# Cross-attention on one NeuronCore: who splits the query and key projections into three bf16 parts

## The chip, the cores and the metric

The kernel runs on one core of one Trainium2 chip. The metric is the time of one execution on the device in microseconds (us). Five engines work side by side, each through its own list of instructions in order: PE (TensorE, matrix products, with its weight loads shown apart as PEld), DVE (VectorE), ACT (ScalarE), POOL (GpSimd) and SP (SyncE, which here only issues DMAs). They meet at semaphores: an instruction may wait until a semaphore has reached a value, and raises one when it ends.

## What is computed

Four cross-attentions share one query: 128 batch elements, 128 queries and 128 keys each, 320 channels in 20 heads of 16. The keys of an element fall into four segments (77, 4, 4 and 43 long), each with its own key and value weights and its own softmax.

```python
q = _heads(hidden_states @ to_q_w)
h_txt = _sdpa(q, _heads(ehs_txt @ to_k_w), _heads(ehs_txt @ to_v_w))
h_obj = _sdpa(q, _heads(ehs_obj @ to_k_object_w), _heads(ehs_obj @ to_v_object_w))
h_oth = _sdpa(q, _heads(ehs_oth @ to_k_others_w), _heads(ehs_oth @ to_v_others_w))
h_ip = _sdpa(q, _heads(ehs_ip @ to_k_ip_w), _heads(ehs_ip @ to_v_ip_w))
out = _merge(h_txt) + _merge(h_obj) + _merge(h_oth) + _merge(h_ip)
out = out @ to_out_w + to_out_b + residual
```

`_sdpa` is softmax(q k^T / 4) v per head.

## The kernel before

**Groups and slots.** Four batch elements form a group (32 groups); the 80 heads of a group are taken eight at a time, an octet, in ten slots. PE, DVE, ACT and POOL each have a function `slot(g, n)` that writes out by hand what the engine does in slot n of group g, and `groups` runs it over all groups. In slot n PE computes the scores of octet n+2 (L824), transposes the probabilities of octet n-2 in two halves into one of two ring banks (L851), multiplies values (L864) and projects the output, which the text calls y (L871). DVE takes maxima, subtracts them, sums the exponentials and inverts the sums (L624, L640, L667, L678). ACT takes the exponentials (L541) and copies the transposed probabilities out of the ring (L550). POOL scales the probabilities (`scale`, L463 and L466).

**Projection jobs.** Beside this PE works twelve jobs a turn (`SEQ`) into two PSUM banks that alternate (`job_ps`): q0 to q2 (queries), kv0 to kv4 (keys, then values) and v0 to v3 (transposes). `PIECES` says in which slot a job or half of one is put: kv0 ends in slot 7, kv1 begins in slot 8, in the same bank. `wait_bank` (L756) makes PE wait until that bank has been read. The jobs q0, q1, q2, kv0, kv1, kv2 (`SPLITS`) of a turn belong to the group two turns later, the other jobs to the next one.

**The three parts.** Queries and keys are multiplied in bf16, each value as a sum of three bf16 parts. For each of the six split jobs of a turn:

- ACT, in `evacuate` (L505): rounds the bank to the first part (L523), and raises `part1_made`. It first waits until the parts buffer, one of three, has been stored (`parts_stored`, L522).
- DVE, in `subtract_part` (L649): bank minus first part into `rest` (L657), and raises `part_freed`, which is what PE waits for (L763) before it writes the bank again.
- POOL, in `split` (L436): adds zero to `rest`, rounded to the second part (L444), then subtracts that for the third part (L447), and raises `part3_made`.
- SP, in `store_parts` (L311): waits for `part3_made` and issues three DMAs that store the parts in DRAM scratch. `load_pair` (L324) waits until all six stores of a group are in, then loads the stacked operands of half a group into `q_all` and `k_all`.

A job that ends in slot m at place 0 (`at` is 0 in `ENDS`) is evacuated by ACT in slot m, one at place 1 in slot m+1; DVE subtracts in slot m+1 and POOL splits in slot m+2, at either place.

**The start.** Before the groups every engine goes through `EARLY_JOBS`: the six split jobs of turn -2 (for group 0), then the twelve jobs of turn -1: kv3, kv4, q0, v0, q1, v1, q2, v2, kv0, v3, kv1, kv2 (splits for group 1). SP's list there, in order: the loads, the stores of the parts 0 to 2 of group 0, `w_o`, the stores of the parts 3 to 5 (L371), `load_pair(0, 0, 0)` (L373), the load of the next context (`load_c(1)`, L374), the store of `small_scr`, 2.6 MB of small key segments (L376), `load_small(1)`, which waits until that store has landed (L378), `load_pair(0, 0, 1)` (L379), two residual loads, `load_x(2)`, and the stores of the parts 0 to 3 of group 1 (L383).

Of the kernel before, what the change touches and what calls it, by code (L numbers as in the profile page):

```python
# [14 lines left out]
P = 128  # L15
# [24 lines left out]
N_CONSTS = 5  # L40
# [85 lines left out]
def split_rows(n):  # L126
    return CT if SPLITS[n][1] == 2 else P
# [7 lines left out]
def xattn_kernel(nc: bass.Bass, x, xT, cT, cT_small, wq, wk, wv, wko, wvo, wkt, wvt, wki, wvi, wo, bo, out):  # L135
# [13 lines left out]
    with ExitStack() as stack:  # L149
# [23 lines left out]
        zero = sb("zero", [P, 1])  # L173
        parts = sb("parts", [P, PR, 3, NB * S], bf16)
        rest = sb("rest", [P, 2, NB * S])
# [45 lines left out]
        part_freed = sem("part_freed")  # L221
        copy_freed = sem("copy_freed")
        part1_made = sem("part1_made")
        part2_made = sem("part2_made")
# [198 lines left out]
        def _(pool):  # L423
# [3 lines left out]
            pool.memset(zero[:, :], 0.0).then_inc(consts_made, 1)  # L427
# [8 lines left out]
            def split(g, n):  # L436

                r = split_rows(n)
                src, dst = rest[0:r, n % 2, :], parts[0:r, n % PR, :, :]
                pool.wait_ge(part_freed, g * NSP + n + 1)  # L440

                after(pool, parts_stored[n % PR], (g * (NSP // PR) + n // PR) * STORED)

                pool.tensor_tensor(dst[:, 1, :], src, zero[0:r, :].broadcast_to((r, NB * S)), ALU.add)\  # L444
                    .then_inc(part2_made, 1)
                pool.wait_ge(part2_made, g * NSP + n + 1)
                pool.tensor_tensor(dst[:, 2, :], src, dst[:, 1, :], ALU.subtract).then_inc(part3_made, 1)  # L447
# [30 lines left out]
            for n in range(3):  # L478
                split(0, n)
            for k in range(CX):  # L480
                x_low(1, k)
            for n in range(3, NSP):
                split(0, n)
            for n in range(NSP):
                split(1, n)
# [3 lines left out]
            def slot(g, n):  # L489

                if live(g * NO + n - 1, G * NO):
                    scale(g if n else g - 1, (n - 1) % NO)
                for at in range(2):
                    for turn, job in ended(g, n - 2, at):
                        if job in SPLITS:
                            split(turn + 2, SPLITS.index(job))
                for k in range(CX):
                    if XLO_AT[k] == n and live(g + 3, G):
                        x_low(g + 3, k)
# [4 lines left out]
        def _(act):  # L504
            def evacuate(turn, job):  # L505

                kind, i = job
                g = turn + shift_of(job)
                ps = job_ps[bank_of(turn, job)]
                act.wait_ge(job_filled, job_count(turn, job))  # L510
                if kind == "v":

                    after(act, v_spread, (g - 1) * NB + i + 1)
                    act.activation(v_new[:, i, :], ps[:, P - CT:3 * P], ACT.Copy).then_inc(copy_freed, 1)
                elif job in COPIES:
                    act.activation(vT[:, i - 2, :, :], ps[:, :].rearrange("p (b t) -> p b t", b=NB), ACT.Copy)\
                       .then_inc(copy_freed, 1)
                else:
                    m = SPLITS.index(job)
                    r = split_rows(m)  # L520

                    after(act, parts_stored[m % PR], (g * (NSP // PR) + m // PR) * STORED)  # L522
                    act.activation(parts[0:r, m % PR, 0, :], ps[0:r, :], ACT.Copy).then_inc(part1_made, 1)  # L523
                    if job == ("kv", 2):

                        act.activation(vT[CT:P, 0, :, :], ps[CT:P, :].rearrange("p (b t) -> p b t", b=NB), ACT.Copy)\
                           .then_inc(v_head_copied, 1)

# [48 lines left out]
            act.wait_ge(pads_made, N_PADS)  # L577
            for turn, job in EARLY_JOBS:
                evacuate(turn, job)
                if (turn, job) == (-2, ("q", 2)):  # L580
                    for k in range(CX):
                        x_high(1, k)
            spread(0, 0)
# [4 lines left out]
            def slot(g, n):  # L588
# [3 lines left out]
                for turn, job in ended(g, n - 1, 1):  # L592
                    evacuate(turn, job)
                for at, (nn, kind, what) in enumerate(FILLS):
# [19 lines left out]
        def _(dve):  # L614
# [34 lines left out]
            def subtract_part(turn, job):  # L649

                g, m = turn + 2, SPLITS.index(job)
                r = split_rows(m)
                ps = job_ps[bank_of(turn, job)]
                dve.wait_ge(part1_made, g * NSP + m + 1)

                after(dve, part3_made, g * NSP + m - 1)
                dve.tensor_tensor(rest[0:r, m % 2, :], ps[0:r, :], parts[0:r, m % PR, 0, :], ALU.subtract)\  # L657
                   .then_inc(part_freed, 1)

# [44 lines left out]
            for turn, job in EARLY_JOBS:  # L704
# [8 lines left out]
                if job in SPLITS:  # L713
                    subtract_part(turn, job)
# [5 lines left out]
            def slot(g, n):  # L720
# [7 lines left out]
                for at in range(2):  # L728
                    for turn, job in ended(g, n - 1, at):
                        if job in SPLITS:  # L730
                            subtract_part(turn, job)
# [10 lines left out]
        def _(pe):  # L742
# [13 lines left out]
            def wait_bank(turn, job):  # L756

                before = previous_in_bank(turn, job)
                if before is not None:
                    t, other = before  # L760
                    g = t + shift_of(other)
                    if other in SPLITS:
                        pe.wait_ge(part_freed, split_count(g, other))  # L763
# [188 lines left out]
```

## Time and profile before

| | |
|---|---|
| median of 3 runs | 1751.53 us (1750.83 to 1751.56) |
| the profiled execution | 1750.32 us |
| its span, first to last instruction | 1748.5 us |
| mean granted clock of PE | 0.990 |
| DMA queue of SP | 365.79 MB, 82.4% of 16 engines' span |

Time is read from the start of the span. A line of the timeline gives start, duration, engine, line and operation, output<-inputs, their shapes and the count, and in brackets the idle time before it with what ended it. A row of waits gives who waited for whom, the total in us, the number of times and the longest.

### The profile page before, as it was taken

Reading aid. Unit: us, or ns where it says so; the run is one execution under the profiler, and the core shown is the slowest. Engines: PE = TensorE matmul, PEld = TensorE weight load, DVE = VectorE, ACT = ScalarE, POOL = GpSimd, SP = SyncE. Lnnn points to the kernel's source line nnn. Section 1 sums busy time; section 2 is a strip of 40 time slices with the busy share of each in tenths; the row PEclk is TensorE's granted clock in tenths of the full one; section 3 lists DMA queues with packets and bytes.
Section 4 is the critical chain, followed back from the end, with each engine's and each line's share of the span. In section 5 each row is a group of like instructions: output and inputs, shape, how many; then the busy total and the mean of one; then the engine's idle time right before and its main releaser. Section 6 shows DMA issues by size and latency. Waiting matters only on the chain.

```text
span 1748.5 us, 48271 instructions
## 1 busy us (share of the span) xinstructions
PE 1663.6 (95%) x15120; PEld 1370.2 (78%) x15120; DVE 1509.1 (86%) x3536; ACT 1042.8 (60%) x1860; POOL 1247.9 (71%) x1452
## 2 busy tenths in 40 slices
PE   6949999999999999999999999999999999999986
PEld 3647888888888888888888888888888888888865
DVE  4238999889999988999998899999889999988997
ACT  1126666666666666666666666666666666666664
POOL 4337777778777777877777887777788777778744
PEclk9979999999999999999999999999999999999999
DMA  8669888888988988898898889889889988987861
GB/s 294 173 168 222 205 221 220 216 219 217 227 201 221 222 215 216 220 224 204 220 224 213 213 222 222 205 222 226 211 213 225 218 208 220 227 209 195 214 128 39
DMA packets 409172, 366.24 MB, mean 209 GB/s; under 512 B 17137, under 2 KB 380210, under 8 KB 404786
## 3 DMA queue, kind: packets, MB, share of 16 engines
q1 hardware_dynamic: 409138, 365.79, 82.4%
q8 instruction: 20, 0.33, 0.1%
q14 instruction: 14, 0.11, 0.0%
HBM read 216.30 MB, written 149.42 MB: 209 GB/s over the span
## 4 chain that ended last, share of the span: by engine, by line
PE 88%; DVE 5%; issue 2%; DMA 1%; ACT 1%; SPq 1%; POOL 1%; ACTq 0%; POOLq 0%
PE job_ps L785 30%; PE ring_ps L851 15%; PE ring_ps L871 12%; PE ring_ps L864 10%; PE job_ps L801 7%; PE s_ps L824 7%; PE job_ps L804 2%; PE ring_ps L752 2%; PE job_ps L812 2%; DVE rest L657 1%; PE job_ps L795 1%; DVE l_seg L667 1%; ACT parts L523 1%; DVE probs L640 1%; DVE m_seg L624 1%
## 5 line engine op out<-in xcount | busy, mean ns | idle before, releaser
L463 POOL TENSOR_TENSOR probs<-probs,rl 128x616 f32<-128x616 f32 (+1 forms) x640 | 628.5, 1004 | 342.1 <-DVE rl L678 340.8
L785 PE MATMUL job_ps<-c_in,w_kv 128*128 128x172 f32 (+1 forms) x2560 | 576.7, 368 | 40.8 <-DVE rest L657 40.8
L550 ACT ACTIVATE pT<-ring_ps 128x512 f32<-128x512 f32 x640 | 378.2, 598 | 356.1 <-PE ring_ps L851 347.3
L785 PEld LDWEIGHTS job_ps<-c_in,w_kv 128*128 128x128 f32 x2560 | 424.4, 190 | 129.8 <-DVE rest L657 48.4
L851 PE MATMUL ring_ps<-ident,probs 128*128 128x128 f32 x2560 | 388.7, 277 | 9.7 <-DVE y L687 8.4
L667 DVE TENSOR_REDUCE l_seg<-probs 128x8 f32<-128x616 f32 (+1 forms) x640 | 385.2, 644 | 7.8 <-ACT probs L541 7.8
L640 DVE TENSOR_TENSOR probs<-s_ps,m_seg 128x616 f32<-128x616 f32 (+1 forms) x640 | 387.5, 647 | 0.0
L624 DVE TENSOR_REDUCE m_seg<-s_ps 128x8 f32<-128x616 f32 (+1 forms) x640 | 371.6, 623 | 3.5 <-issue 0.2
L541 ACT ACTIVATE probs<-probs 128x1024 f32<-128x1024 f32 x320 | 337.7, 1055 | 22.8 <-DVE probs L644 22.8
L851 PEld LDWEIGHTS ring_ps<-ident,probs 128*128 128x128 f32 x2560 | 290.0, 143 | 64.9 <-issue 25.6
L444 POOL TENSOR_TENSOR parts<-rest,zero 128x512 bf16<-128x512 f32 (+1 forms) x192 | 199.0, 1036 | 70.6 <-DVE rest L657 70.6
L657 DVE TENSOR_TENSOR rest<-job_ps,parts 128x512 f32<-128x512 f32 (+1 forms) x192 | 131.4, 684 | 127.0 <-ACT parts L523 127.0
L871 PE MATMUL ring_ps<-w_o,oT 128*128 128x320 f32 x768 | 231.9, 438 | 5.7 <-ACT pT L550 5.0
L447 POOL TENSOR_TENSOR parts<-rest,parts 128x512 bf16<-128x512 f32 (+1 forms) x192 | 222.3, 1158 | 15.0
L824 PE MATMUL s_ps<-k_all,q_all 128*128 128x128 bf16 x2560 | 196.0, 219 | 6.4 <-DVE probs L644 6.4
L824 PEld LDWEIGHTS s_ps<-k_all,q_all 128*128 128x128 bf16 x2560 | 165.4, 101 | 42.3 <-issue 27.5
L864 PE MATMUL ring_ps<-pT,v_pad 128*32 128x128 f32 x5120 | 194.8, 277 | 0.0
L871 PEld LDWEIGHTS ring_ps<-w_o,oT 128*128 128x128 f32 x768 | 135.8, 190 | 53.1 <-ACT pT L550 11.6
L864 PEld LDWEIGHTS ring_ps<-pT,v_pad 128*32 128x32 f32 x5120 | 159.8, 110 | 14.1 <-issue 0.8
L557 ACT ACTIVATE oT<-ring_ps 128x256 f32<-128x256 f32 x128 | 49.2, 384 | 199.3 <-PE ring_ps L864 195.7
L523 ACT ACTIVATE parts<-job_ps 128x512 bf16<-128x512 f32 (+1 forms) x192 | 113.5, 591 | 86.4 <-PE job_ps L795 44.7
L801 PE MATMUL job_ps<-x_hi,w_q 128*128 128x512 f32 x384 | 145.6, 420 | 19.5 <-POOL x_lo L452 15.4
(47 smaller groups left out, 1457.0 us busy)
## 6 DMA issues: line engine op xcount, KB each, us to landing
q_all<-q_scratch SPq DMA_DIRECT2D x64, 960.0 KB, 8.4
k_all<-k_scratch SPq DMA_DIRECT2D x64, 960.0 KB, 12.4
c_in<-in_cT SPq DMA_DIRECT2D x32, 1024.0 KB, 5.1
x_raw<-in_xT SPq DMA_DIRECT2D x32, 768.0 KB, 5.1
q_scratch<-parts SPq DMA_DIRECT2D x64, 384.0 KB, 3.0
k_scratch<-parts SPq DMA_DIRECT2D x64, 384.0 KB, 3.0
x_res<-in_x SPq DMA_DIRECT2D x128, 160.0 KB, 3.4
out<-y SPq DMA_DIRECT2D x128, 160.0 KB, 2.8
```

Source lines behind the costliest of these rows:

```text
L463: pool.tensor_tensor(pr[:, :, a:e], pr[:, :, a:e], r[:, :, s:s + 1].broadcast_to((P, OH, e - a)), ALU.mult)
L541: act.activation(pr, pr, ACT.Exp, scale=SCALE).then_inc(exp_done, 1)
L550: act.activation(pT[:, h:h + QH, :], ring_ps[i][:, :].rearrange("p (h s) -> p h s", h=QH), ACT.Copy)\
L624: dve.tensor_reduce(m_seg[:, o % 2, :, k:k + 1], sc[:, :, a:e], axis=AX.X, op=ALU.max)\
L640: dve.tensor_tensor(pr[:, :, a:e], sc[:, :, a:e], m_seg[:, o % 2, :, k:k + 1].broadcast_to((P, OH, e - a)), ALU.subtract)
L667: dve.tensor_reduce(l_seg[:, o % 2, :, s:s + 1], pr[:, :, a:e], axis=AX.X, op=ALU.add)
L785: last = pe.matmul(dst[:, :, a:e], w_kv[:, l, k, i * P:(i + 1) * P], c_in[:, k, :, a:e], start=(k == 0), stop=(k == CK - 1))
L801: pe.matmul(ps[:, :], w_q[a][:, k, i * P:(i + 1) * P], (x_hi, x_lo)[c][:, k, :], start=(k == 0 and (a, c) == (0, 0)), stop=False)
L824: last = pe.matmul(s_ps[o % 2][:, i * T:(i + 1) * T], q_st[s // 2][:, h, s % 2, :], k_st[s // 2][:, h, s % 2, :], start=True, stop=True)
L851: last = pe.transpose(ring_ps[i][:, k * S:(k + 1) * S], probs[:, (o % NR) * OH + q * QH + k, :], ident[:, :])
L864: last = pe.matmul(ring_ps[i][a * VW:(a + 1) * VW, k * S:(k + 1) * S], v_pad[:, s, h, :], pT[:, (s % 2) * H + h, :], start=(e == 0), stop= ...
L871: last = pe.matmul(ring_ps[i][:, 0:C], oT[:, k, :], w_o[:, k, :], start=(k == 0), stop=(k == 2))
```

## The change

The difference is now taken on POOL, from a copy of the bank that ACT makes in SBUF (`whole`, fp32), and the second part is rounded by ACT. The bank is free as soon as ACT has made the copy and the first part. `split` on POOL becomes `make_rest` and `make_third`, with `round_second` of ACT between them. POOL calls `make_rest` one slot after ACT's evacuation, and `make_third` one slot later, in the same slot as ACT's `round_second`. At the start ACT rounds the second part of a split job after it has evacuated the split job that follows.

```diff
-            def split(g, n):
+            def make_rest(g, n):
                 r = split_rows(n)
-                src, dst = rest[0:r, n % 2, :], parts[0:r, n % PR, :, :]
-                pool.wait_ge(part_freed, g * NSP + n + 1)
-                after(pool, parts_stored[n % PR], (g * (NSP // PR) + n // PR) * STORED)
-                pool.tensor_tensor(dst[:, 1, :], src, zero[0:r, :].broadcast_to((r, NB * S)), ALU.add)\
-                    .then_inc(part2_made, 1)
+                src = whole[0:r, n % 2, :]
+                pool.wait_ge(part1_made, g * NSP + n + 1)
+                pool.tensor_tensor(src, src, parts[0:r, n % PR, 0, :], ALU.subtract).then_inc(rest_made, 1)
+
+            def make_third(g, n):
+                r = split_rows(n)
                 pool.wait_ge(part2_made, g * NSP + n + 1)
-                pool.tensor_tensor(dst[:, 2, :], src, dst[:, 1, :], ALU.subtract).then_inc(part3_made, 1)
+                pool.tensor_tensor(parts[0:r, n % PR, 2, :], whole[0:r, n % 2, :], parts[0:r, n % PR, 1, :],
+                                   ALU.subtract).then_inc(part3_made, 1)
...
-            for n in range(3):
-                split(0, n)
-            for k in range(CX):
-                x_low(1, k)
-            for n in range(3, NSP):
-                split(0, n)
-            for n in range(NSP):
-                split(1, n)
+            for g in range(2):
+                for n in range(NSP):
+                    if (g, n) == (0, 3):
+                        for k in range(CX):
+                            x_low(1, k)
+                    make_rest(g, n)
+                    make_third(g, n)
...
                 for at in range(2):
-                    for turn, job in ended(g, n - 2, at):
+                    for turn, job in ended(g, n - 2 - at, at):
                         if job in SPLITS:
-                            split(turn + 2, SPLITS.index(job))
+                            make_third(turn + 2, SPLITS.index(job))
+                for at in range(2):
+                    for turn, job in ended(g, n - 1 - at, at):
+                        if job in SPLITS:
+                            make_rest(turn + 2, SPLITS.index(job))
...
+                    after(act, part3_made, g * NSP + m - 1)
+                    act.activation(whole[0:r, m % 2, :], ps[0:r, :], ACT.Copy)
+
                     after(act, parts_stored[m % PR], (g * (NSP // PR) + m // PR) * STORED)
                     act.activation(parts[0:r, m % PR, 0, :], ps[0:r, :], ACT.Copy).then_inc(part1_made, 1)
...
+            def round_second(g, m):
+                r = split_rows(m)
+                act.wait_ge(rest_made, g * NSP + m + 1)
+                act.activation(parts[0:r, m % PR, 1, :], whole[0:r, m % 2, :], ACT.Copy).then_inc(part2_made, 1)
...
+            waiting = None
             for turn, job in EARLY_JOBS:
                 evacuate(turn, job)
+                if job in SPLITS:
+                    if waiting is not None:
+                        round_second(*waiting)
+                    waiting = (turn + 2, SPLITS.index(job))
                 if (turn, job) == (-2, ("q", 2)):
                     for k in range(CX):
                         x_high(1, k)
+            round_second(*waiting)
             spread(0, 0)
...
                 for turn, job in ended(g, n - 1, 1):
                     evacuate(turn, job)
+                for at in range(2):
+                    for turn, job in ended(g, n - 2 - at, at):
+                        if job in SPLITS:
+                            round_second(turn + 2, SPLITS.index(job))
...
-                dve.tensor_tensor(rest[0:r, m % 2, :], ps[0:r, :], parts[0:r, m % PR, 0, :], ALU.subtract)\
-                   .then_inc(part_freed, 1)
...
                     if other in SPLITS:
-                        pe.wait_ge(part_freed, split_count(g, other))
+                        pe.wait_ge(part1_made, split_count(g, other))
```

With `subtract_part` its two calls on DVE go, and so do the column `zero` and its memset.

## Rows read from the trace of the kernel before

**Rows 1.** The page, part 1: busy time, share of the span, instructions
```profile
PE 1663.6 (95%) x15120; PEld 1370.2 (78%) x15120; DVE 1509.1 (86%) x3536; ACT 1042.8 (60%) x1860; POOL 1247.9 (71%) x1452
```

**Rows 2.** Who waited for whom, 140 to 1640 us, PE, then PEld
```profile
PE job_ps L785 <- DVE rest L657: 19.8, 29, 0.7
...
PEld ring_ps L871 <- ACT pT L550: 4.8, 30, 0.2
```

**Rows 3.** Timeline of PE, 895 to 955 us: scores of octet 0, kv1, y
```profile
923.47 0.61 PE L824 MATMUL s_ps<-k_all,q_all 128*128 128x128 bf16 x8
...
925.21 2.34 PE L785 MATMUL job_ps<-c_in,w_kv 128*128 128x308 f32 x8 [0.68 <-DVE rest L657]
...
927.82 1.78 PE L871 MATMUL ring_ps<-w_o,oT 128*128 128x320 f32 x6
```

**Rows 4.** The chain that ended last, 0 to 140 us: start, length, what
```profile
74.88 14.07 DMA small_scratch<-probs
...
106.80 0.61 ACT parts L523
...
108.18 5.09 PE job_ps L785 x16
...
122.86 1.12 DVE l_seg L667 x2
```

**Rows 5.** Timeline of POOL, 0 to 135 us: the last third part of group 0
```profile
56.34 1.15 POOL L447 TENSOR_TENSOR parts<-rest,parts 64x512 bf16<-64x512 f32 x1
```

**Rows 6.** Timeline of ACT, 0 to 135 us
```profile
76.43 0.60 ACT L523 ACTIVATE parts<-job_ps 128x512 bf16<-128x512 f32 x1 [1.33 <-PE job_ps L804]
...
117.77 0.59 ACT L523 ACTIVATE parts<-job_ps 64x512 bf16<-64x512 f32 x1 [3.73 <-PE job_ps L795]
...
119.00 0.83 ACT L566 ACTIVATE v_pad<-v_new 128x320 f32<-128x320 f32 x2
...
121.30 1.04 ACT L541 ACTIVATE probs<-probs 128x1024 f32<-128x1024 f32 x1
```

**Rows 7.** Timeline of ACT, 895 to 955 us
```profile
923.35 0.60 ACT L550 ACTIVATE pT<-ring_ps 128x512 f32<-128x512 f32 x1 [1.18 <-PE ring_ps L851]
923.84 0.59 ACT L523 ACTIVATE parts<-job_ps 128x512 bf16<-128x512 f32 x1
924.32 0.63 ACT L535 ACTIVATE x_hi<-x_raw 128x512 fp32r<-128x512 f32 x1
...
926.10 0.61 ACT L550 ACTIVATE pT<-ring_ps 128x512 f32<-128x512 f32 x1
```

**Rows 8.** Timeline of SP, 0 to 135 us
```profile
50.61 8.65 SPq L322 DMA_DIRECT2D k_scratch<-parts  x9
61.13 0.36 SPq L330 DMA_DIRECT2D q_all<-q_scratch  x1
61.53 0.88 SPq L330 DMA_DIRECT2D k_all<-k_scratch  x1
...
74.49 0.35 SPq L295 DMA_DIRECT2D c_in<-in_cT  x1
```

**Rows 9.** Busy time by stretch; the last columns are granted clock, DMA share, GB/s
```profile
65.00:69.00 4.00, 4.00 (x13) 2.15 (x12) 1.39 (x2) 0.00 (x0) 0.00 (x0) 1.00 1.19 203
...
72.00:75.00 3.00, 3.00 (x18) 2.63 (x17) 0.00 (x0) 0.50 (x1) 0.00 (x0) 1.00 0.08 12
75.00:79.00 4.00, 2.92 (x15) 2.17 (x14) 0.69 (x1) 1.02 (x3) 1.09 (x2) 1.00 0.76 225
```

**Rows 10.** Costliest groups of instructions, shapes apart: a subtraction on POOL
```profile
L452 POOL TENSOR_TENSOR x_lo<-x_raw,x_hi 128x512 fp32r<-128x512 f32 x96 | 122.1, 1275 | 55.3 <-ACT x_hi L535 55.2
```

**Rows 11.** Who waited for whom, 140 to 1640 us, all engines
```profile
POOL probs L463 <- DVE rl L678: 293.2, 177, 2.9
```

**Rows 12.** Timeline of SP, 895 to 955 us: a load of the key stack
```profile
901.62 3.26 SPq L330 DMA_DIRECT2D k_all<-k_scratch  x1
```

**Rows 13.** The line L330, 140 to 1600 us: from issue to landing
```profile
DMA to landing us min/median/max: 7.1/10.5/14.0
```

More of the change, by code:

```diff
@@ L39 @@
 N_SMALL = len(SMALL) * MKV
-N_CONSTS = 5
+N_CONSTS = 4
 N_PADS = 6
@@ L172, in xattn_kernel @@
         ident = sb("ident", [P, P])
-        zero = sb("zero", [P, 1])
         parts = sb("parts", [P, PR, 3, NB * S], bf16)
-        rest = sb("rest", [P, 2, NB * S])
+        whole = sb("whole", [P, 2, NB * S])
         q_all = sb("q_all", [P, NPAIR * H * 2 * S], bf16)
@@ L220, in xattn_kernel @@
         job_filled = sem("job_filled")
-        part_freed = sem("part_freed")
         copy_freed = sem("copy_freed")
         part1_made = sem("part1_made")
+        rest_made = sem("rest_made")
         part2_made = sem("part2_made")
@@ L426, in _ @@
                 pool.memset(t[:, :, C:3 * P].bitcast(fp32), 0.0).then_inc(consts_made, 1)
-            pool.memset(zero[:, :], 0.0).then_inc(consts_made, 1)
             pool.memset(ident[:, :], 0.0).then_inc(consts_made, 1)
@@ L647, in shift @@
                    .then_inc(shifted, 1)
[L649 to L656, printed above, removed]
-                dve.tensor_tensor(rest[0:r, m % 2, :], ps[0:r, :], parts[0:r, m % PR, 0, :], ALU.subtract)\
-                   .then_inc(part_freed, 1)
             def sum_up(g, o):
@@ L712, in _ @@
                     reduce_max(0, 0)
-                if job in SPLITS:
-                    subtract_part(turn, job)
             dve.wait_ge(small_stored, 16)
@@ L727, in slot @@
                         add_residual(g + what // NB, what % NB, at % 2)
[L728 to L731, printed above, removed]
                 if live(gg, G):
```

## The prediction

> **What bounds the kernel now.** First the shares of the page: PE is busy 95% of the span, DVE 86%, POOL 71%, ACT 60% [rows 1]. So only what PE waits for can give time back. Second, who waits for whom in the steady part, 140 to 1640 us: PE's matmuls wait for one thing alone, the subtraction on DVE, 29 times and 19.8 us in all, 0.68 us each [rows 2]. The timeline shows the place: in slot 8, kv1 may not write its bank until DVE has read kv0 out of it [rows 3]. This is the largest gain that the steady part can hold: 19.8 us, 1.1% of the time. Third, the start: there the chain runs for long stretches through DMAs and SP's list, not through PE: the store of `small_scr` lands at 74.88 + 14.07 = 88.95 us, what SP has queued behind it brings in the first store of group 1's query parts, and at 106.80 ACT can at last overwrite that buffer, after which DVE subtracts, and PE goes on with kv1 at 108.18 [rows 4]. Anything that makes SP late there is paid in full.
>
> **The change, part by part.** I write the group index first, so (0, 5) is the last split job of group 0.
>
> *A, SP's list at the start.* ACT now rounds the second part of (0, 5) only after it has evacuated the next split job, and that is q0 of the next turn. Before, POOL had its third part at 56.34 + 1.15 = 57.49 [rows 5]. Now ACT's evacuation of q0 begins at 76.43 [rows 6]; whole copy, first part and rounding take, at the spacing of 0.48 between two of ACT's copies [rows 7], 2 x 0.48 + 0.63 = 1.6, so to 78.0; a wake of some 0.05 (the gap between dependent steps of SP, 74.49 + 0.35 to 74.88 [rows 4, 8]) and the subtraction's 1.15 [rows 5] make 79.2. SP's list waits there: in front of it the store of (0, 5), behind it `load_pair(0, 0, 0)`, `load_c(1)`, `small_scr`, `load_small(1)`. Before, the pair was issued 61.13 - 57.49 = 3.64 after the third part [rows 5, 8], so it is now issued at 82.9, 21.8 later. That alone is not the delay, for `load_c` waited until 74.49 for a job of PE [rows 8]. Behind the pair's issue, 61.53 + 0.88 - 61.13 = 1.3 us [rows 8], it now comes at 84.3: 9.8 later. The store of `small_scr` follows directly, and before it found an empty queue: between 72 and 75 us the DMA share was 0.08 [rows 9]. Now the pair's 2 x 960 KB lie in front of it. The pair took from 61.13 to 72.2 (0.08 of the last 3 us), 11.1 us, so now to 94.0. Then the context and `small_scr`, 74.49 to 88.95 before, 14.46; of this some 1.4 was start-up, which the share of 0.76 beside 1.19 in 4 us shows [rows 9], and is hidden when they queue. So the store lands at 94.0 + 13.0 = 107.0, 18.1 later. Bounds: 84.3 + 14.46 = 98.8 if the pair took nothing from it (9.8 later), 108.5 if nothing is hidden (19.5 later). I take 18.1, because the pair kept the engines as full (1.19) as anything does [rows 9].
>
> What follows the store to 106.80 is the same list, loads and buffer: so ACT's first part of kv0 begins at 124.9. PE's kv0 needs the late context too, which by the above is in by some 101, and stays in that shadow.
>
> The Trainium skill ("DMA: Bandwidth & Descriptors", section Bandwidth) puts the HBM side's limit for one core at about 358 GB/s. By that figure the pair's 1.97 MB would be an estimated 5.5 us and the store would land 5.6 earlier than I say. The trace does not agree: the pair moves at 203 GB/s with the engines full [rows 9], and the sum goes by that.
>
> *B, the release of the bank at that point.* The whole copy is made while ACT waits for the buffer. From the start of the first part to PE it was 108.18 - 106.80 = 1.38 [rows 4]; now it is the part's 0.61 and a wake: -0.7.
>
> *C, the end of the start.* After kv2 ACT had first part and a second copy, and went on with `spread` at 119.00, 1.23 after 117.77 [rows 6]. Now it makes whole copy and first part (0.48 more), rounds (1, 4) (0.5 to 0.6), then has to wait for the rest of (1, 5), which POOL makes only after the third part of (1, 4): third 1.15, rest between 1.15 and 1.28 [rows 5, 10], and the wakes; then it rounds (1, 5), 0.6. With wakes 0.48 + 0.6 + 0.05 + 1.15 + 0.05 + 1.2 + 0.05 + 0.5, some 4.0, so the first exponential starts at 125.3 instead of 121.30 [rows 6], counted with all else where it was, and is done 1.04 later. DVE's first sum, at 122.86 and in the chain [rows 4], comes at 126.4: +3.6. At least it is 1.0 (two more copies of ACT), at most 4.0.
>
> *D, the steady slots.* Slot 8: ACT's evacuation of kv0 begins at 923.84 and not sooner, since the copy before it has waited 1.18 for PE [rows 7]. Whole copy 0.48, first part 0.60, wake 0.05: PE is released at 924.97 instead of 925.21, 0.24 less [rows 3, 7]. Behind this ACT copies the ring bank that y needs: it began at 926.10 and took 0.61 [rows 7]; whole copy (0.48) and the rounding of q2 (0.5 to 0.63) now stand ahead of it, so it ends at 927.7 to 927.8, and y, which could start at 927.82 - 0.24 = 927.58 [rows 3], waits 0.1 to 0.25. Net -0.1 to 0.05. Slot 6: y already waits there, once a group, 4.8 us in 30 times [rows 2]; q2's evacuation just ahead has one copy more, of which I take 0.1, for ACT too waits for PE there; the bounds are 0 and 0.48. Together +1 over 30 groups, between -7 (0.24 x 30, nothing given back) and +15.
>
> *What I cost at nothing.* DVE loses 192 subtractions (six a group); DVE is not what PE waits for but at that one place. POOL gets a subtraction (1.15 to 1.28) for an addition, and `make_third` waits in POOL's list for ACT; the octet's `scale` and the `x_low` of slots 8 and 9 queue behind it. POOL idles before `scale` 293 us in 30 groups, near 10 a group [rows 11]; without that cover PE's transposes wait. ACT gets two copies for each split, some 1.1 x 192 = 211 us, and its share becomes some 71%; its waits for `rest` and for the third part of two jobs before are met a slot earlier. On SP, the third parts of jobs that end at place 1 come a slot later, and the stores, the output stores and `load_pair` behind them: the later half of the key stack was issued at 901.62 and lands at most 14.0 later, 915.6 [rows 12, 13]; a slot later (at most 1750.32 / 320 slots = 5.5 us) that is 921.1, and the first scores that read it stand at 923.47 [rows 3]. So that is hidden too, with 2 us to spare.
>
> **Sum**, against the profiled execution of 1750.32: 18.1 - 0.7 + 3.6 + 1.0 = 22.0, so 1772.3. The median of the runs shown is 1.2 above that execution: **1773.5 us**, 1.3% slower.
>
> **The rivals.**
> 1. *The queued transfers overlap.* If the pair costs the store less than its full time, the store lands between 98.8 and 107.0. For it: small and large transfers share the engines. Against it: the share is full while the pair runs [rows 9]. The time is 1751.5 + 9.8 - 0.7 + 3.6 + 1.0 = 1765 at the lower end. By the figure of the Trainium skill that A names, an estimate, it would be 1768.
> 2. *The gap in slot 8 closes altogether* (the other side). Its place is PE's wait before kv1; it decides if ACT's two copies end by 924.5, where PE would otherwise stand, 0.45 sooner than my reading. Price -19.8 [rows 2]. With A at its lower bound and C at 1.0 that gives 9.8 - 0.7 + 1.0 - 19.8 = -9.7, 1742 us. Against it: the copy ahead waits for PE's transposes [rows 7], so nothing can start the two copies sooner.
> 3. *ACT's copies come too late for PE in every group.* In slots 6 and 8 y waits for a ring bank; at 0.5 us a group instead of 0.03 this is +15 in place of +1: 1787.5. For it: both slots are at their limit [rows 2, 7]. Against it: ACT itself waits for PE in them.
> That the change does not do what it says is no rival: the order of ACT's list at the start can be read from the code.
>
> **How the numbers follow.** Forecast 0.60 (1766 to 1780 with its own bounds), rival 1 0.17, rival 2 0.05, rival 3 0.15, and 0.03 for a gain and a loss that cancel. The range has to reach to most of rivals 1 and 3: 1757 to 1788. A measurement of this kernel tells 0.2%, 3.5 us, from no change; faster is rival 2, slower all but rival 2 and the cancelling.
>
> **What would show it.** A: the pair issued near 83 instead of 61.13, `small_scr` landing near 107, kv1's first matmul at 125 to 126. B: kv1 released by ACT's first part. C: first exponential about 7.5 us after kv2's evacuation begins, not 3.5. D: the wait in slot 8 is put down to ACT, 0.4 to 0.5 a group. I am wrong if the pair is issued before 75 us, or if the distance from kv1 at the start to the end of the span changes by over 15 us.

## The result, and the profile after

The changed kernel takes **1766.09 us** (median; 1765.38 to 1766.72), the kernel before 1751.3 beside it: a ratio of 1.0085, 95% interval 1.0067 to 1.0102. That is +14.8 us, where +22.0 was forecast; it lies in the range, on its faster side. The span is 1763.4 us, 14.9 longer than before.

Part 1 of the page after [rows 1]:

```profile
PE 1674.5 (95%) x15120; PEld 1373.2 (78%) x15120; DVE 1393.6 (79%) x3344; ACT 1211.7 (69%) x2244; POOL 1265.9 (72%) x1451
```

The work moved as the diff says: DVE lost 115.5 us of busy time and 192 instructions, ACT gained 168.9 us and 384, POOL 18. And the time grew: at most places PE waits for none of the three. The few where it does come next.

**The start.** Timeline of SP after, 0 to 150 us [rows 8]:

```profile
82.54 0.36 SPq L329 DMA_DIRECT2D q_all<-q_scratch  x1
82.95 0.88 SPq L329 DMA_DIRECT2D k_all<-k_scratch  x1
83.87 5.59 SPq L294 DMA_DIRECT2D c_in<-in_cT  x1
```

The chain that ended last, after, 0 to 140 us [rows 4]:

```profile
77.80 1.17 POOL parts L445
...
89.50 14.76 DMA small_scratch<-probs
...
119.84 0.61 ACT parts L528
...
120.49 5.48 PE job_ps L789 x16
...
139.08 1.21 DVE l_seg L677 x2
```

The pair is issued at 82.54 instead of 61.13, after the late third part of (0, 5) at 77.80. Behind it SP stands 5.59 us in the issue of `c_in` alone, which took 0.35 before [rows 8]: the queue holds the pair. The store of `small_scr` lands at 89.50 + 14.76 = 104.26, 15.3 later than before; kv1 begins 12.3 later (120.49 for 108.18), DVE's first sum 16.2 later (139.08 for 122.86).

Busy time by stretch, after; the last three columns are granted clock, DMA share and GB/s [rows 9]:

```profile
88.00:90.00 2.00, 0.00 (x0) 0.00 (x0) 0.00 (x0) 0.00 (x0) 0.00 (x0) 0.50 1.24 249
90.00:92.00 2.00, 0.00 (x0) 0.00 (x0) 0.00 (x0) 0.00 (x0) 0.00 (x0) 0.50 1.30 252
```

At little more share of the engines (1.24 and 1.30 beside 1.19) the pair now moves at some 250 GB/s, where before it was 203 [rows 9]; from 86 to 88 us it is 270, but the first stretch of a load is the fastest in e1 too (249, then 199). Nothing in the forecast accounts for that. Loads from issue to landing, before and then after (number, KB, us):

```profile
k_all<-k_scratch SPq DMA_DIRECT2D x1, 960.0 KB, 11.7
...
c_in<-in_cT SPq DMA_DIRECT2D x1, 1024.0 KB, 5.9
```

```profile
c_in<-in_cT SPq DMA_DIRECT2D x1, 1024.0 KB, 12.6
...
k_all<-k_scratch SPq DMA_DIRECT2D x1, 960.0 KB, 11.2
```

The pair, whose second half is `k_all`, lands at 82.95 + 11.2 = 94.2, the context at 83.87 + 12.6 = 96.5. So the context comes in 2.3 us behind the pair, where alone it took 5.9, and `small_scr` lands 10.1 us behind the pair.

Timeline of ACT after, 0 to 145 us [rows 6]:

```profile
130.47 0.59 ACT L525 ACTIVATE whole<-job_ps 64x512 f32<-64x512 f32 x1 [2.73 <-PE job_ps L799]
...
135.19 0.63 ACT L538 ACTIVATE parts<-whole 64x512 bf16<-64x512 f32 x1 [2.37 <-POOL whole L439]
...
138.01 1.99 ACT L552 ACTIVATE probs<-probs 128x1024 f32<-128x1024 f32 x2
```

From kv2's evacuation to the first exponential it is 138.01 - 130.47 = 7.54 us, where before it was 3.53; 2.37 of them ACT waits for POOL's last `rest`.

**The steady slots.** Who waited for whom after, 150 to 1655 us (total, times, longest) [rows 2]:

```profile
PE job_ps L789 <- ACT parts L528: 13.0, 29, 0.4
PEld ring_ps L875 <- ACT pT L561: 12.9, 59, 0.2
```

The wait before kv1 fell from 19.8 to 13.0; the wait of y's weight loads for a ring bank rose from 4.8 to 12.9, and comes twice a group instead of once. Timelines of slot 8 after, PE and then ACT [rows 3, 7]:

```profile
939.59 2.34 PE L789 MATMUL job_ps<-c_in,w_kv 128*128 128x308 f32 x8 [0.45 <-ACT parts L528]
...
942.35 1.88 PE L875 MATMUL ring_ps<-w_o,oT 128*128 128x320 f32 x6
```

```profile
937.96 0.60 ACT L561 ACTIVATE pT<-ring_ps 128x512 f32<-128x512 f32 x1 [1.18 <-PE ring_ps L855]
938.46 0.59 ACT L525 ACTIVATE whole<-job_ps 128x512 f32<-128x512 f32 x1
938.93 0.60 ACT L528 ACTIVATE parts<-job_ps 128x512 bf16<-128x512 f32 x1
...
941.19 0.63 ACT L538 ACTIVATE parts<-whole 64x512 bf16<-64x512 f32 x1
941.71 1.29 ACT L561 ACTIVATE pT<-ring_ps 128x512 f32<-128x512 f32 x2
```

ACT's two copies end at 939.53 and PE follows after 0.45 idle (0.68 before); q2's rounding at 941.19 then stands ahead of the ring copy that y reads, and six matmuls of y take 1.88 instead of 1.78. Octets are counted from the start, ten to a group. ACT's exponential of octet 20 begins at 234.40 us for 220.34 before, that of octet 290 at 1614.45 for 1599.33: 14.1 and 15.1 late, so 27 groups cost 1.1 us together. So nearly all of the +14.8 is the start.

In between, group 0 makes some 2 us of the start's 16.2 good: the exponential of octet 10 is 14.0 late (183.29 for 169.27). The waits of PE before, 121 to 180 us, show two that are gone after; that these are what is made good is argued from their size, not shown:

```profile
PE job_ps L801 <- DVE rest L657: 1.9, 1, 1.9
PE job_ps L785 <- DVE rest L657: 0.7, 1, 0.7
```

### The profile page after: what moved, and what is told of

It reads as the page before. It is cut to its first block, busy times and chain, and to the rows that moved or that the text cites. A ratio compares the mean times of both kernels' runs of the same rounds, so it can differ in the third digit from the quotient of the medians.

```text
span 1763.4 us, 48140 instructions
## 1 busy us (share of the span) xinstructions
PE 1674.5 (95%) x15120; PEld 1373.2 (78%) x15120; DVE 1393.6 (79%) x3344; ACT 1211.7 (69%) x2244; POOL 1265.9 (72%) x1451
## 4 chain that ended last, share of the span: by engine, by line
PE 89%; DVE 4%; ACT 2%; issue 2%; DMA 1%; SPq 1%; POOL 0%; ACTq 0%; POOLq 0%
PE job_ps L789 30%; PE ring_ps L855 15%; PE ring_ps L875 12%; PE ring_ps L868 10%; PE job_ps L805 7%; PE s_ps L828 7%; PE job_ps L808 2%; PE job_ps L816 2%; PE ring_ps L756 2%; PE job_ps L799 1%; ACT parts L528 1%; DVE l_seg L677 1%; DMA small_scratch<-probs 1%; DVE probs L661 1%; DVE m_seg L645 1%
## 5 line engine op out<-in xcount | busy, mean ns | idle before, releaser
L445 POOL TENSOR_TENSOR parts<-whole,parts 128x512 bf16<-128x512 f32 (+1 forms) x192 | 222.2, 1157 | 236.9 <-ACT parts L538 233.2
L439 POOL TENSOR_TENSOR whole<-whole,parts 128x512 f32<-128x512 f32 (+1 forms) x192 | 222.1, 1157 | 6.4 <-ACT parts L528 6.4
L875 PEld LDWEIGHTS ring_ps<-w_o,oT 128*128 128x128 f32 x768 | 135.6, 190 | 61.2 <-ACT pT L561 19.7
L525 ACT ACTIVATE whole<-job_ps 128x512 f32<-128x512 f32 (+1 forms) x192 | 113.6, 592 | 81.9 <-PE job_ps L799 64.5
L805 PE MATMUL job_ps<-x_hi,w_q 128*128 128x512 f32 x384 | 144.2, 416 | 17.0 <-DVE oT L705 15.3
L451 POOL TENSOR_TENSOR x_lo<-x_raw,x_hi 128x512 fp32r<-128x512 f32 x96 | 121.9, 1273 | 7.2 <-ACT x_hi L546 7.0
```

The lines of the kernel that those rows point to most:

```text
L805: pe.matmul(ps[:, :], w_q[a][:, k, i * P:(i + 1) * P], (x_hi, x_lo)[c][:, k, :], start=(k == 0 and (a, c) == (0, 0)), stop=False)
L875: last = pe.matmul(ring_ps[i][:, 0:C], oT[:, k, :], w_o[:, k, :], start=(k == 0), stop=(k == 2))
```

## The experiments

Each edit is made to the changed kernel unless another is named. Ratios are to the kernel before, run beside it: it took 1751.3 us beside the change, 1751.38 beside e1 to e4, 1750.49 beside e5 to e8 and 1751.27 beside e9 to e12.

**Why were the loads faster?** The change drops a column `zero` of 4 bytes a partition; what is allocated behind it moves. One kernel keeps it:

```diff
+        zero = sb("zero", [P, 1])      # unused, at its old place
```

> The changed kernel with the unused 4-byte column `zero` still allocated where it was, so that all buffers behind it in SBUF (parts, whole, q_all, k_all, ...) stand as in the kernel before. Nothing else differs. Theory placement: the key and query stack loads were faster after the change (250 to 270 GB/s beside 195 to 203 before at the start) because their destination moved by those 4 bytes. Then here the pair moves at about 200 GB/s again, DMA share in the middle of the kernel is 0.86 instead of 0.78, kv1 starts near 125.5 us instead of 120.5, and the time is about 5 us above the changed kernel's 1766.1, 1771. Rival, traffic: the loads were faster because less else was in the queues at that time. Then the rate stays at 250 to 270 GB/s and the time at 1766.

1770.82 us, 1.0108 (1.0093 to 1.0123): 4.7 slower than the change without it. Stretches, and the chain:

```profile
88.00:90.00 2.00, 0.00 (x0) 0.00 (x0) 0.00 (x0) 0.00 (x0) 0.00 (x0) 0.89 1.18 199
90.00:92.00 2.00, 0.00 (x0) 0.00 (x0) 0.00 (x0) 0.00 (x0) 0.00 (x0) 0.50 1.20 181
```

```profile
90.99 15.86 DMA small_scratch<-probs
...
124.25 0.61 ACT parts L529
```

```profile
k_all<-k_scratch SPq DMA_DIRECT2D x1, 960.0 KB, 12.5
```

The pair is back at 181 to 199 GB/s, so the placement makes the difference in rate. The store lands at 106.85 and ACT's first part of kv0 begins at 124.25; forecast were 107.0 and 124.9. But this execution issued the pair at 83.83, 1.3 later than the change did, and such a difference is found without any move of the buffers (e11, placed like the change and with the same start, issues it at 83.48). So of the 4.4 us between 119.84 and 124.25 some 3.1 are left for the placement. And the agreement with the forecast is made of errors that cancel; the section on why the prediction was right or wrong has them.

Against the kernel before, whose buffers stand at the same places, the change costs 1770.82 - 1751.38 = 19.4 us, and not 14.8.

The reverse: the kernel before, with `zero` allocated behind `y` instead of at its place.

> The kernel before with `zero` allocated behind all other buffers. Nothing else differs. Theory placement: the pair moves at 250 to 270 GB/s, DMA share in the middle 0.78 instead of 0.86; at the start the pair that stands ahead of group 1's first parts takes 2 to 3 us less, kv1 starts near 106 instead of 108.2, and the time falls by 2 to 3 us to 1749; the steady groups keep their 51.07 us, since no engine waits for these loads there. Rival, traffic: the rate stays at 200 GB/s and the time at 1751.3.

1748.85 us, 0.9986 (0.9977 to 0.9995). Stretches, and the chain:

```profile
65.00:69.00 4.00, 4.00 (x13) 2.04 (x12) 1.65 (x2) 0.00 (x0) 0.00 (x0) 1.00 1.25 241
```

```profile
107.13 6.15 PE job_ps L785 x16
...
122.87 1.12 DVE l_seg L667 x2
```

The loads speed up as expected, 241 GB/s where it was 203, but the gain at the start falls short: kv1 comes 1.05 sooner, and DVE's first sum not at all (122.87 for 122.86). The first pair is not waited for here, since `c_in` waits for PE until 74.97 anyway. What the second pair gains is lost to PE's clock: kv1's 16 matmuls take 6.15 us for 5.09 before. Stretches before, then of this kernel (the granted clock is the third number from the end):

```profile
111.00:113.00 2.00, 2.00 (x12) 1.68 (x11) 0.00 (x0) 0.00 (x0) 0.00 (x0) 0.90 0.82 317
```

```profile
111.00:113.00 2.00, 2.00 (x10) 1.82 (x9) 0.00 (x0) 0.00 (x0) 0.00 (x0) 0.62 0.67 252
```

In both PE had been idle, for 19.29 us before and 17.81 here, and began kv1 at a granted clock of 0.50, the lower of its two levels (1.2 GHz); here it stays there longer. The traces of the two kernels end 0.8 us apart (1748.5 and 1747.7), nearly all of it from the steady groups: the exponential of octet 20 is 0.04 sooner, that of octet 290 0.77. The rest of the 2.4 us that the medians show lies in no trace. A faster transfer pays only where it is waited for: in the changed kernel it is. Against this kernel, whose column is out of the way like the change's, the change costs 1766.09 - 1748.85 = 17.2 us.

**Is it the late third part of (0, 5)?** It is rounded at once, before the jobs of turn -1:

```diff
                     waiting = (turn + 2, SPLITS.index(job))
+                if (turn, job) == (-2, ("kv", 2)):
+                    round_second(*waiting)
+                    waiting = None
```

> The changed kernel, but at the start ACT rounds the second part of (0, 5) before it goes on to turn -1, and not after q0 of turn -1. Theory A (SP is held by the store of (0, 5), and all behind it is late): the pair is issued near 66 us instead of 82.5, `small_scr` lands near 89 instead of 104.3, kv1 starts near 105 instead of 120.5, and the time falls by about 15 us to 1751. Rival (the start is late because ACT has two copies more per job and POOL waits for ACT each time): kv1 comes no more than 3 us sooner, and the time stays above 1762.

1751.56 us, 1.0003 (0.9994 to 1.0012): 14.5 of the 14.8 are gone. Timeline of SP:

```profile
66.78 0.36 SPq L329 DMA_DIRECT2D q_all<-q_scratch  x1
...
74.63 0.35 SPq L294 DMA_DIRECT2D c_in<-in_cT  x1
```

The pair is issued before the context's release again, so its issue no longer holds anything up. Part A is nearly the whole loss. Against e2, where the buffers are moved as here, 2.7 us are left (1751.56 for 1748.85), for the parts C and D.

**Is it the issue that is late, or the transfers in front?** The pair is issued behind the store instead of ahead of it: `load_pair(0, 0, 0)` moves from before `load_c(1)` to before `load_small(1)`.

> The changed kernel, but SP issues the first load of the stacks behind the store of `small_scr` instead of ahead of it. Theory queue (what delays group 1's first parts is all that stands ahead of them in one queue, in whatever order): `small_scr` lands some 7 us sooner, near 97, but kv1 starts where it did, 120.5 within 2 us, because the pair now stands in front of the second pair. Rival (the wait for `small_scr` to land is what counts): kv1 starts some 7 us sooner, near 113.5, and the time falls to 1759.

1763.14 us, 1.0063 (1.0048 to 1.0079). Timeline of SP, and the chain:

```profile
83.82 8.34 SPq L329 DMA_DIRECT2D q_all<-q_scratch  x1
```

```profile
82.65 13.81 DMA small_scratch<-probs
...
118.33 6.12 PE job_ps L789 x16
```

The store lands at 96.46, 7.8 sooner, so the pair did stand in front of it. But kv1 comes only 2.2 sooner and the time is 3.0 shorter: the pair then delays what follows, 8.34 us in one issue. In these two runs another order within the full queue shifts the delay, and only the earlier issue (e3) removes it.

**Part C: the last rounding ahead of the first exponential.** `round_second(*waiting)` moves behind the `spread`s and the `x_high` copies.

> The changed kernel, but at the end of the start ACT makes the last rounding, of (1, 5), after the two spreads and the three high parts, not before them. Theory C (ACT waits there 2.4 us for POOL's rest, and the first exponential behind it is late): the wait is gone, the first exponential starts 2.4 us sooner after kv2's evacuation, 5.1 instead of 7.5, and the time falls by 2 to 2.5 us to 1763.8. Rival (the first group makes it up anyway, since DVE has less to do there): the exponential is sooner, but the time stays within 1 us of 1766.1.

1764.27 us, 1.0077 (1.0063 to 1.009): 1.8 less by the medians, 1.0 less against the kernel before beside each, and the two intervals overlap. Timeline of ACT:

```profile
130.15 0.59 ACT L525 ACTIVATE whole<-job_ps 64x512 f32<-64x512 f32 x1 [2.73 <-PE job_ps L799]
...
135.41 1.99 ACT L552 ACTIVATE probs<-probs 128x1024 f32<-128x1024 f32 x2
```

The first exponential begins 135.41 - 130.15 = 5.26 after kv2's evacuation instead of 7.54; some 1.7 over the 3.53 of before stay. But the exponential of octet 20 begins at 233.61 for 234.40, only 0.8 sooner. So what ACT is late here is paid in part, and group 0 makes up the greater part: the result lies between the theory and the rival.

**Part D: q2's rounding ahead of y's ring copy in slot 8.** It moves behind that copy:

```diff
-                        if job in SPLITS:
+                        if job in SPLITS and n != 8:
                             round_second(turn + 2, SPLITS.index(job))
...
+                        if n == 8 and what[1] == 0:
+                            for turn, job in ended(g, n - 3, 1):
+                                if job in SPLITS:
+                                    round_second(turn + 2, SPLITS.index(job))
```

> The changed kernel, but in slot 8 ACT rounds q2's second part behind the first copy out of the ring and not ahead of it. Theory D (kv1 is released 0.23 us sooner in every group, but y in slot 8 then waits for that ring copy, which the rounding has made late): PE's wait for the ring copies, put on its weight loads at 12.9 us in the middle of the kernel, falls to near the 4.8 of the kernel before, a group takes 0.15 to 0.25 us less, and the time falls by 4 to 7 us to 1760.5. Rival (y's ring copy is not what holds PE there): the time stays at 1766.

1759.18 us, 1.0048 (1.0035 to 1.0062): 6.9 less, 6.1 against the kernel before beside each. Waits, 150 to 1655 us:

```profile
PE job_ps L793 <- ACT parts L528: 13.4, 30, 0.4
...
PEld ring_ps L879 <- ACT pT L561: 6.5, 30, 0.2
```

The wait before kv1 stays as it was, the wait of y halves from 59 times to 30. So the gain of the sooner release was really there, 6 to 7 us, and y in slot 8 had taken it.

All three mends together:

> The changed kernel with the three orders mended: the second part of (0, 5) rounded before turn -1 (as in the run that rounds it at once), the last rounding of the start behind the high parts, and slot 8 as in the run on its order. If A, C and D are separate, their gains add: 1751.6 - 2.3 - 5.5, about 1744, 0.4% below the kernel before. If the first group makes C up, 1746; if slot 8 gives nothing, 1749 to 1751.

1743.41 us, 0.9959 (0.9945 to 0.9973). Singly they gave 14.5, 1.8 and 6.9, in sum 23.2; together 22.7. Against the kernel before beside each it is 14.6, 1.0 and 6.1, in sum 21.7; together 21.9. The three parts add, as expected. Of the 7.1 us by which this kernel beats the one before, some 2.5 are the column's (e2).

**Was DVE's relief worth anything?** The subtractions' time is given back to DVE as work that nobody uses, one instruction for each split job in its old slot:

```diff
+                            dve.tensor_tensor(spare[:, 1, :], spare[:, 0, :], spare[:, 0, :], ALU.subtract)
```

> The changed kernel, with one more subtraction of 512 columns on DVE for each split job, at the place where it stood before, from and into spare buffers that nobody waits for. Theory (DVE's relief is worth nothing, since PE waits for DVE at that one place alone): DVE's busy share goes from 79% back to about 86%, and the time stays within 2 us of 1766.1. Rival (the relief of DVE hides part of what ACT's longer list costs): the time rises by more than 3 us.

1809.52 us, 1.0334 (1.0319 to 1.035). A miss: I had expected no change. The added instruction by its tile (count, then ns: min, median, max), and one group of POOL's scalings, in the changed kernel and here (busy us, mean ns):

```profile
L741 DVE TENSOR_TENSOR spare<-spare x180: 735/744/4330, 156.0 to 1710.6; 128x512 f32<-128x512 f32 x180
```

```profile
L462 POOL TENSOR_TENSOR probs<-probs,rl 128x344 f32<-128x344 f32 x320 | 248.3, 776 | 0.0
```

```profile
L463 POOL TENSOR_TENSOR probs<-probs,rl 128x344 f32<-128x344 f32 x320 | 302.7, 946 | 0.0
```

Half of them take at most 744 ns, one takes 4330, and POOL's 344-wide scaling rises from 776 to 946 ns mean. One that begins at 976.17 and takes 4.05 us runs beside two of POOL's scalings. The old subtraction had one input in PSUM, this one two in SBUF. So the run does not test DVE's load but a collision. The same with one input, a reduction of the same 128x512 by maximum:

```diff
+                            dve.tensor_reduce(spare[:, 1, 0:1], spare[:, 0, :], axis=AX.X, op=ALU.max)
```

> The changed kernel with one more instruction on DVE for each split job, at the same place as in the run that loads DVE, but a maximum over 512 columns with one input in SBUF, in place of a subtraction with two. In that run the added instruction took 0.74 us where POOL was idle and up to 4.05 where POOL was busy, and POOL's own multiplications beside it 2.41 instead of 1.96. Theory port (an instruction of DVE with two inputs in SBUF and one of POOL shut each other out; DVE's load as such costs nothing): here the added instruction takes about 0.7 us everywhere, DVE is busy some 86%, and the time stays within 3 us of 1766.1. Rival (DVE's time is what counts): it is as slow as that run, above 1790.

1765.85 us, 1.0085 (1.0069 to 1.01): the time of the change to 0.3 us, with DVE busy 1498.1 us (85%).

```profile
L741 DVE TENSOR_REDUCE spare<-spare x180: 673/676/678, 154.0 to 1665.0; 128x1 f32<-128x512 f32 x180
```

Every one takes 673 to 678 ns. DVE's 104 us came back and cost nothing, so their going had been worth nothing. The Trainium skill (GPSIMD Engine Reference, section Specifications) says that POOL shares its SBUF interfaces with VectorE, with contention for DVE instructions that have two SBUF inputs; the two runs agree (up to 4330 ns with two inputs, 678 with one). They differ in what they write as well, 512 columns against one, so that it is the inputs is not shown apart.

**More on where buffers lie.** On the three-mended kernel, 128 unused bytes a partition ahead of the parts buffers (`pad = sb("pad", [P, 32])`):

> The kernel with the three mended orders and 128 unused bytes ahead of the parts buffer, so that all that stands behind it moves by 128 bytes; without them the stacks stand at a multiple of 64 bytes by the sizes of the buffers ahead, with them at another. Theory 1 (any start on 64 bytes is as good): the loads of the stacks keep their 240 to 275 GB/s, and the time stays at 1743.4 within 1.5 us. Theory 2 (a start on 256 bytes is better still): the share of the DMA engines falls below 0.75 in the middle, and the time by 1 to 3 us, at the start alone.

1745.85 us, 0.9971 (0.9959 to 0.9983): 2.4 slower than without by the medians, 1.7 against the kernel before beside each, with intervals that overlap; a miss for both readings. Stretches of this kernel, then of the three-mended one:

```profile
96.00:98.00 2.00, 0.00 (x0) 0.00 (x0) 0.00 (x0) 0.00 (x0) 0.00 (x0) 0.50 1.21 200
```

```profile
96.00:98.00 2.00, 0.00 (x0) 0.00 (x0) 0.00 (x0) 0.00 (x0) 0.00 (x0) 0.50 1.25 242
```

200 GB/s instead of 242 at nearly the same share (from 94 to 96 us 214 instead of 247), and from 400 to 1600 us a share of 0.84 instead of 0.79: the place matters for a move of 128 bytes too. That it is the rate that costs the time is argued. The rule stays open. The Trainium skill (DMA: Bandwidth & Descriptors, section How a descriptor splits into AXI transactions) says that a descriptor which doesn't start at a multiple of 256 bytes costs extra; no trace here shows the addresses, so this is not settled.

**Could the gap before kv1 have closed (rival 2)?** In slot 7 ACT evacuates kv0 ahead of the second ring copy instead of behind it:

```diff
+                    if n == 7 and kind == "tr" and what[1] == 0:
+                        for turn, job in ended(g, n, 0):
+                            evacuate(turn, job)
...
                 for turn, job in ended(g, n, 0):
-                    evacuate(turn, job)
+                    if n != 7:
+                        evacuate(turn, job)
```

> The changed kernel, but in slot 7 ACT evacuates kv0 ahead of the second copy out of the ring and not behind it; kv0 is done before the transposes that this copy waits for. Theory (what is left of the gap before kv1, 0.45 us a group, comes from the place of the evacuation in ACT's list): PE waits no more for ACT before kv1, and the time falls by 13 us, the 13.0 of the row of waits, and the slack of the weight loads behind it, to 1747 to 1753. Rival (y in slot 8 waits for the same ring copy as before, so the gain is given back): less than 5 us.

1751.58 us, 1.0001 (0.9992 to 1.0011): 14.5 less, the start's loss made good in the slots. Timeline of ACT in slot 7, and the waits, 150 to 1640 us:

```profile
929.40 0.60 ACT L525 ACTIVATE whole<-job_ps 128x512 f32<-128x512 f32 x1 [0.71 <-PE job_ps L803]
929.90 0.59 ACT L528 ACTIVATE parts<-job_ps 128x512 bf16<-128x512 f32 x1
930.37 0.60 ACT L561 ACTIVATE pT<-ring_ps 128x512 f32<-128x512 f32 x1
```

```profile
PEld ring_ps L879 <- ACT pT L561: 19.9, 59, 0.5
```

The bank of kv0 is full before the second half of the transposes, and ACT had stood idle there, waiting for PE. Now PE never waits before kv1 (that row is gone); the later ring copies give some of it back at y, whose weight loads wait 19.9 us for 12.9.

Everything together, and in slot 6 q2's evacuation behind the first ring copy, for y:

> The kernel with the three mended orders, kv0 first in slot 7 as in the run on it, and in slot 6 q2 evacuated behind the first copy out of the ring. If the gains add: 1743.4 - 13 for the gap - 6.5 for the wait of y in slot 6 that is left, some 1724 to 1728, 1.4% below the kernel before. If the wait in slot 6 is PE's own order: 1730. If PE then waits for something else (scores behind DVE, or POOL's scaling), it stops between 1735 and 1743.

**1720.15 us** (1719.4 to 1721.64), 0.9825 (0.9811 to 0.9838). It beats both kernels: 1.75% under before (1.6% under e2, which has its placement), 2.6% under the change, and is 4 us better than I expected. 400 to 1600 us by engine:

```profile
400.00:1600.00 1200.00, 1200.00 (x11272) 1008.23 (x11271) 1025.22 (x2491) 897.33 (x1675) 943.83 (x1079) 1.00 0.80 221
```

In the same 1200 us the three-mended kernel has PE busy for 1189.26 with 11078 recorded matmuls. The idle time that went explains 0.9%. From octet 20 to octet 290 ACT's exponentials take 1352.7 us for 1373.25 there, 1.5% less; so the rest lies in how closely PE's work follows on itself, and is not shown further.

## Why the prediction was right or wrong

**A, direction and path right, the term too large.** Pair issued at 82.54 (forecast 82.9), `load_c` reached at 83.87 (84.3), the pair landed at 94.2 (94.0), and e3 shows that this is nearly the whole loss. Two steps behind it were too long by 5.1 us together:

- "Of this some 1.4 was start-up", so 13.0 from the pair to the landing of `small_scr`. It was 10.1, so 4.4 of the 14.46 are hidden, because the context comes in 2.3 us behind the pair. In e1 it is the same 10.1 (84.23 + 12.5 = 96.7 to 106.85), so the placement is not the reason. The reading of the pair was off as well: by its own row it landed at 61.53 + 11.7 = 73.2 before, not at 72.2.
- "What follows the store to 106.80 is the same list": 15.58 us, not 17.85, so ACT's first part of kv0 came at 119.84 instead of 124.9. With the column kept (e1) it is 17.40. The second pair stands in this stretch, and its `k_all` took 10.1 us to land, for 12.4 before and 11.9 in e1. Here the rate of before, 203 GB/s, was carried over to a kernel in which the buffers behind the column move by its 4 bytes. The diff shows the column go; the prediction gave that no price at all.

That e1 with 106.85 and 124.25 meets the forecast is luck: its pair was issued 0.9 later than forecast and landed 12.9 us after its issue instead of 11.1, which hides the first error.

**B, right.** kv1 starts 120.49 - 119.84 = 0.65 after the first part begins; 0.61 and a wake were forecast, 1.38 before.

**C, right at its place, but not paid in full.** 7.54 us to the first exponential, forecast 7.5. Taking 2.3 of it away (e5) brought 1.0 to 1.8.

**Left out: group 0 recovers.** The sum carried the delay at DVE's first sum, 16.2 as measured, through to the end. By octet 10 it is 14.0. In e3, where A is gone, the first exponential is 2.9 late (124.23 for 121.30) and that of octet 10 not at all (169.24 for 169.27): there group 0 takes up the whole of C. The two waits of before, 1.9 and 0.7 us for `rest`, would account for most of it; that is not shown.

**D, right.** Waits of PE for ACT in place of DVE, 0.45 instead of 0.68 before kv1, given back at y in slot 8: +1.1 over 27 groups, forecast +1. e6 shows both halves apart. The placement helps here too: with the column kept (e1) they cost 2.1 (the exponentials are 19.7 late at octet 20 and 21.8 at octet 290), so that the size agrees so well is in part luck.

**What was costed at nothing** held: kv0 was ready at 102.23 in the shadow of the buffer's wait, POOL and SP in the slots cost nothing that the waits show, and DVE's relief is worth nothing (e9). ACT's busy time grew by 168.9 us, not by 211.

**The rivals.** 1 (1765 to 1768) came nearest in time, and in part for its reason: the store landed between 98.8 and 107.0, as it says, because the context comes in close behind the pair; the rest is the faster second pair. The limit of 358 GB/s that the Trainium skill gives (DMA: Bandwidth & Descriptors, section Bandwidth) was not reached by the pair; the most that a stretch of it shows is 270, from 86 to 88 us. Other loads passed it, 385 GB/s from 101 to 103 us before, and there the measurement decides. 2 did not happen in this kernel, but my ground against it, that "nothing can start the two copies sooner", was wrong: another order of ACT's list can (e11), and it is worth 14.5 us. 3 did not happen: y's extra wait is 8.1 us by its row, about as much as kv1's wait gave.

## What to carry to other kernels

An instruction that moves back in one engine's list is priced by who waits behind it in another's: here one rounding on ACT, of 0.6 us, held SP's whole list for 21 us. A transfer rate read from a trace belongs to the place of its buffer; if a change allocates more or less, keep the old layout in one run before the rate is trusted, or the time: here the moved buffers hid 2.4 to 4.7 us of what the change costs. And where an engine copies late "because it waits for PE", look at what it waits for: the copy that is ready first should stand first, which was worth 14.5 us here (e11), as much as the start lost.

## What the runs showed of the hardware

- The same loads from DRAM, 1.97 MB at a DMA share of 1.2, moved, behind their first stretch, at 181 to 214 GB/s or at 231 to 266, according to a move of the buffers by 4 or by 128 bytes. Over 400 to 1600 us the share for the same 217 GB/s is 0.86 before, 0.78 after and 0.80 in e2.
- A subtraction on DVE with two SBUF inputs and POOL's work hold each other up: it took 735 to 4330 ns, POOL's 344-wide scaling 946 ns instead of 776, and 180 of them cost this kernel 43 us; a reduction of the same size with one input and one column out took 673 to 678 ns in the same slots.
- The issue of a load on SP took 0.35 us with nothing queued, 5.59 (a context) and 8.34 us (a query load) behind other large transfers; that it waits for room in the queue is the reading of these numbers.
- A context of 1 MB took 5.9 us to land alone, and landed 2.3 us behind the pair when it was queued behind it.
- After 17.81 us idle PE began at a granted clock of 0.50, and 16 matmuls of kv1 took 6.15 us; after 19.29 us idle the same took 5.09, as the clock was back sooner (0.90 for 0.62 between 111 and 113 us).
